# Inverse square roots of an attention kernel's norms: one GpSimd power in place of VectorE's Newton rounds

## What is computed

```python
def rmsnorm(x, g, eps=EPS):                      # cross-attention, D = 128
    var = jnp.mean(jnp.square(x), axis=-1, keepdims=True)
    return x * jax.lax.rsqrt(var + eps) * g
q = rmsnorm((hidden @ Wq).reshape(B, Sq, 16, 128), gq)
k = rmsnorm((context @ Wk).reshape(B, 257, 16, 128), gk)
...
def rms_norm(x):                                 # self-attention, 16 numbers a head
    return x * jax.lax.rsqrt(jnp.mean(x * x, axis=-1, keepdims=True) + RMS_EPS)
q, k = (rms_norm(q), rms_norm(k))                # 16 + 4 heads = 20 norms a row
```

## Time and profile before

| | before |
|---|---|
| median of 3 runs | 1631.33 us |
| profiled execution, its own time | 1639.87 us |
| its span | 1638.0 us |
| PE busy | 1413.0 us, 86% |
| DVE busy | 1067.2 us, 65% |
| ACT busy | 866.7 us, 53% |
| POOL busy | 543.6 us, 33% |
| mean granted TensorE clock | 0.928 |

### The profile page before, as it was taken

The page is one execution under the profiler, slowest core; times in us unless marked ns, Lnnn a source line. Parts: engine busy times, 40 slices in busy tenths (PEclk is TensorE's granted clock), DMA queues, the critical chain, the costliest instruction groups (busy, mean ns, idle before and its releaser), DMA issues.

```text
span 1638.0 us, 32905 instructions
## 1 busy us (share of the span) xinstructions
PE 1413.0 (86%) x9178; PEld 988.4 (60%) x9178; DVE 1067.2 (65%) x3905; ACT 866.7 (53%) x3432; POOL 543.6 (33%) x1338
## 2 busy tenths in 40 slices
PE   5859989999999998989989999999998989955872
PEld 2635757575756666565757575756666665735661
DVE  7737677776768586767777676768586767733112
ACT  4455556556665556565555566665656565521110
POOL 2243343334242425243343334242425243310003
PEclk9989899999999999999898999999999989876896
DMA  9000000000000001010000000000001000100534
GB/s 368 4 24 8 22 20 20 13 26 14 23 17 14 26 10 30 7 30 9 20 20 20 13 24 17 23 17 23 16 10 29 9 28 6 58 6 9 170 125 131
DMA packets 41214, 59.83 MB, mean 37 GB/s; under 512 B 5094, under 2 KB 35953, under 8 KB 40096
## 3 DMA queue, kind: packets, MB, share of 16 engines
q1 hardware_dynamic: 36880, 50.73, 9.8%
q0 software_dynamic: 2064, 6.14, 1.1%
q10 hardware_dynamic: 2176, 2.10, 0.4%
HBM read 48.62 MB, written 10.49 MB: 36 GB/s over the span
## 4 chain that ended last, share of the span: by engine, by line
PE 46%; issue 26%; POOL 12%; ACT 7%; DVE 4%; DMA 3%; POOLq 1%; SPq 0%; DVEq 0%; ACTq 0%
PE AB L587 21%; PE Eb L587 9%; PE Db L587 5%; PE C L704 3%; PE C L587 3%; ACT px L1003 2%; POOL prob L1140 2%; DMA ctxn<-expert_rows 2%; PE AB L783 2%; POOL c_lo L1105 2%; PE C L720 2%; ACT AB L924 2%; POOL pjunk L1099 1%; POOL rstd L1116 1%; POOL rkx L1131 1%
## 5 line engine op out<-in xcount | busy, mean ns | idle before, releaser
L924 ACT ACTIVATE AB<-AB 128x128 f32<-128x128 f32 (+1 forms) x1160 | 303.0, 261 | 203.4 <-PE AB L587 198.6
L1099 POOL TENSOR_TENSOR pjunk<-pjunk 128x1 f32<-128x1 f32 x288 | 57.3, 199 | 653.8 <-DVE sinv L1443 383.6
L1281 DVE BATCH_NORM_STATS2 kst<-AB 128x6 f32<-128x256 f32 x512 | 181.9, 417 | 83.3 <-PE AB L587 49.4
L924 ACT ACTIVATION_READ_ACCUMULATOR AB<-AB 128x1 f32 (+1 forms) x1160 | 215.8, 186 | 0.0
L587 PE MATMUL AB<-wk_hi,c_hi 128*128 128x512 f16 x512 | 203.7, 398 | 11.2 <-DVE wvo_lo L1354 2.9
L587 PE MATMUL AB<-wk_lo,c_hi 128*128 128x512 f16 x512 | 201.9, 394 | 0.0
L587 PE MATMUL AB<-wk_hi,c_lo 128*128 128x512 f16 x512 | 201.0, 393 | 0.0
L993 ACT ACTIVATE prob<-prob,nbias,rq 128x257 f32<-128x257 f32 x256 | 150.7, 591 | 39.8 <-DVE nbias L1438 39.4
L587 PE MATMUL AB<-ctxT,qpT 128*128 128x257 f32 x512 | 140.7, 422 | 0.6 <-DVE kst L1281 0.6
L1140 POOL TENSOR_SCALAR prob<-prob,sinv 128x257 f32<-128x257 f32 x256 | 125.0, 488 | 20.1
L1116 POOL TENSOR_TENSOR rstd<-var,minus_half 128x1 f32<-128x1 f32 x64 | 35.5, 555 | 266.6 <-DVE var L1266 232.1
(11 more groups left out here) (253 smaller groups left out, 3278.0 us busy)
## 6 DMA issues: line engine op xcount, KB each, us to landing
ctxT<-in_ctxT SPq DMA_DIRECT2D x64, 128.5 KB, 2.1
ctxn<-in_ctxn SPq DMA_DIRECT2D x64, 128.0 KB, 2.1
wq_hi<-in_w SPq DMA_DIRECT2D x4, 768.0 KB, 5.2
wq_lo<-in_w SPq DMA_DIRECT2D x4, 768.0 KB, 6.5
expert_rows<-base POOLq DMA_DIRECT2D x1, 2048.0 KB, 15.8
xin<-in_x SPq DMA_DIRECT2D x16, 128.0 KB, 2.2
prob<-in_wqT SPq DMA_DIRECT2D x1, 2048.0 KB, 19.7
xres<-in_x SPq DMA_DIRECT2D x16, 128.0 KB, 2.0
```

The lines of the kernel that those rows point to most:

```text
L924: ins = nc.scalar.activation(k, k, ACT.Square, accum_out=sums[0:m, h:h + 1])
L1099: own.mark(pool.tensor_tensor(pjunk[:, 0:1], pjunk[:, 1:2], pjunk[:, 1:2], ALU.mult))
L1281: ins = V.bn_stats(stats[:, 0, 2 * half + n], AB[0:m, 2 + half, 2 * D * n:2 * D * (n + 1)])
```

## The change

`newton` and its scratch tiles go. DVE still makes mean square plus epsilon, now into tiles of their own (`nk`, `nq`, `nqk`), and signals `norm_ready`. POOL takes it to the power -0.5 in one `tensor_tensor` against a tile filled with -0.5, in four new steps: `p0` and `p1` (128 x 64 each), `pq` (128 x 16) and `pk` (128 x 20); in the first period also one of 64 x 16 in `rkl`. DVE's `RQ` is cut in two: what follows the inverse root (the 16 copies) is the new step `rq`, which waits for `pq` and stands behind `f` (in the first period behind `tw`). `qkv` is cut in the same way; `qr` follows it at once and waits for `pk`.

```diff
 ORDER = {
-    "DVE": """K0 X K1 K2 dp3 XL K3 KN0 do3 Q RQ f K4 K5 qkv K6 s0 sc K7 i0 s1 KN1 pt dp0 i1 pv s2 pr ln2 dp1 lg i2
+    "DVE": """K0 X K1 K2 dp3 XL K3 KN0 do3 Q RQ f rq K4 K5 qkv qr K6 s0 sc K7 i0 s1 KN1 pt dp0 i1 pv s2 pr ln2 dp1 lg i2
               do0 up pos do1 s3 dn dp2 i3 do2""".split(),
-    "POOL": """h0 h1 n3 h2 X cl r0 ln1 c1 c0 r1 c2 h3 n0 r2 n1 y c3 ln2 r3 n2 scat""".split(),
+    "POOL": """h0 h1 n3 h2 X cl p0 r0 pq ln1 c1 c0 r1 c2 h3 pk n0 p1 r2 n1 y c3 ln2 r3 n2 scat""".split(),
 START_ORDER = {
-    "DVE": """low wk KL KNL K0 K1 X K2 XL wql K3 gg KN0 Q W0l wt0 W1l K4 RQ wt1 M01 wt K5 M23 tw s0 s1 i0 K6 dp0
+    "DVE": """low wk KL KNL K0 K1 X K2 XL wql K3 gg KN0 Q W0l wt0 W1l K4 RQ wt1 M01 wt K5 M23 tw rq s0 s1 i0 K6 dp0
-    "POOL": """hl h1 h3 h2 h0 rkl X r0 pz r1 cl c0 n0 c1 n1 r2 c2 r3 n2 c3""".split(),
+    "POOL": """hl h1 h3 h2 h0 rkl X p0 r0 pz pq r1 cl c0 n0 c1 n1 p1 r2 c2 r3 n2 c3""".split(),
...
+            def inverse(p, name, out, src):
+                pool.wait_ge(norm_ready.sem, norm_ready.at(p, name))
+                m, n = src.shape
+                ins = pool.tensor_tensor(out, src, minus_half[0:m, 0:n], ALU.pow)
+                if name in ("RQ", "qkv"):
+                    ins.then_inc(inv_ready.sem, 1)
+                else:
+                    own.mark(ins)
...
-                step(V.tensor_scalar(na[0:m, 0:n], src, 1.0 / (D * WK_SCALE ** 2), X_EPS, ALU.mult, ALU.add))
-                newton(n, out, m).then_inc(rk_ready.sem, 1)
+                V.tensor_scalar(out, src, 1.0 / (D * WK_SCALE ** 2), X_EPS, ALU.mult, ALU.add).then_inc(norm_ready.sem, 1)
...
-                step(newton(H, rqt[:]))
+            def step_rq(p):
+                dve.wait_ge(inv_ready.sem, inv_ready.at(p, "pq"))
                 for b in range(NB):
                     for m in range(4):
...
-                step(newton(NQK, qki[:]))
+            def step_qr(p):
+                dve.wait_ge(inv_ready.sem, inv_ready.at(p, "pk"))
                 step(V.tensor_tensor(qki[:, 0:AH], qki[:, 0:AH], again[:], ALU.mult))
```

More of the change, by code:

```diff
@@ L57 @@
 N_CONST = sum(CONSTS.values())
-DVE_STEPS = dict(pro=80, full=89, last=38, expert=0)
-POOL_STEPS = dict(pro=37, full=40, last=5, expert=0)
+DVE_STEPS = dict(pro=35, full=43, last=26, expert=0)
+POOL_STEPS = dict(pro=40, full=42, last=5, expert=0)
 class Period:
@@ L147 @@
 LATE = {"n3", "ph3", "tl3", "oh3", "pt3", "o3", "dp3", "do3", "f", "ln1", "xt1", "qkv", "qk", "sc", "pt", "pv", "y", "yt", "pr",
-        "ln2", "xt2", "lg", "up", "pos", "dn", "scat"}
+        "ln2", "xt2", "lg", "up", "pos", "dn", "scat", "qr", "pk"}
 ORDER = {
@@ L218, in build @@
         ones = sb("ones", [P, P])
-        minus_half = sb("minus_half", [P, 1])
+        minus_half = sb("minus_half", [P, NB * H])
         wq_hi = sb("wq_hi", [P, KC, INNER], F16)
@@ L328, in build @@
         na = sb("na", [P, NB * H])
-        nb_ = sb("nb_", [P, NB * H])
-        nc_ = sb("nc_", [P, NB * H])
+        nk = sb("nk", [P, 2, NB * H])
+        nq = sb("nq", [P, H])
+        nqk = sb("nqk", [P, AH + AKV])
         tscale = sb("tscale", [P, 10], BF16)
@@ L380, in build @@
                              full=entries("POOL", FULL, "h"))
-        rk_ready = Events(sem("rk_ready"), pro=steps_among("DVE", PRO, ["KNL", "KN0", "KN1"]),
-                          full=steps_among("DVE", FULL, ["KN0", "KN1"]))
+        norm_ready = Events(sem("norm_ready"), pro=steps_among("DVE", PRO, ["KNL", "KN0", "KN1", "RQ"]),
+                            full=steps_among("DVE", FULL, ["KN0", "KN1", "RQ", "qkv"]), last=["qkv"])
+        inv_ready = Events(sem("inv_ready"), pro=["pq"], full=steps_among("POOL", FULL, ["pq", "pk"]), last=["pk"])
         rq_ready = Events(sem("rq_ready"), **fills)
@@ L1115, in rsqrt @@
                 pool.wait_ge(var_ready.sem, var_ready.at(p, name))
-                pool.tensor_tensor(rstd[:, n:n + 1], var[:, n:n + 1], minus_half[:], ALU.pow)\
+                pool.tensor_tensor(rstd[:, n:n + 1], var[:, n:n + 1], minus_half[:, 0:1], ALU.pow)\
                     .then_inc(rstd_ready.sem, 1)
+            def inverse(p, name, out, src):
[6 more added lines that the diff above has]
+                    own.mark(ins)
             def spread(p, b):
-                pool.wait_ge(rk_ready.sem, rk_ready.at(p, "KN0" if b < 2 else "KN1"))
                 if p.kind == "pro":
@@ L1200, in step_rkl @@
             def step_rkl(p):
-                pool.wait_ge(rk_ready.sem, rk_ready.at(p, "KNL"))
+                inverse(p, "KNL", rkl[:], nk[0:BATCH, 1, 0:H])
+                own.settle()
                 pool.tensor_copy(rkx[0:BATCH, 0, 0].rearrange("p (h q) -> p h q", q=SQ),
@@ L1206, in _ @@
                      "ln2": lambda p: rsqrt(p, "ln2", 3), "pz": step_pz, "scat": scatter,
-                     "hl": step_hl, "rkl": step_rkl, "cl": split_last}
+                     "hl": step_hl, "rkl": step_rkl,
+                     "p0": lambda p: inverse(p, "KN0", all_of(rk[:, 0:NB]), nk[:, 0]),
+                     "p1": lambda p: inverse(p, "KN1", all_of(rk[:, NB:2 * NB]), nk[:, 1]),
+                     "pq": lambda p: inverse(p, "RQ", rqt[:], nq[:]), "pk": lambda p: inverse(p, "qkv", qki[:], nqk[:]), "cl": split_last}
             for b in range(NB):
@@ L1244, in gate @@
                 own.mark(V.memset(junk[:], 0.0))
[L1246 to L1258, removed]
             def layer_norm(p, name, n, x, out, free=None):
@@ L1305, in step_KN @@
                 n = NB * H
-                key_norms(p, P, n, kst[:, NB * part:NB * (part + 1)], kn2[:, n * part:n * (part + 1)], all_of(rk[:, NB * part:NB * (part + 1)]),
-                          f"KN{part}")
+                key_norms(p, P, n, kst[:, NB * part:NB * (part + 1)], kn2[:, n * part:n * (part + 1)], nk[:, part], f"KN{part}")
             def step_X(p):
@@ L1323, in step_RQ @@
                 sums_from_stats(P, qst[:], 1, qn2[:])
-                step(V.tensor_scalar(na[:, 0:H], qn2[:], 1.0 / (D * WQ_SCALE ** 2), X_EPS, ALU.mult, ALU.add))
-                step(newton(H, rqt[:]))
+                V.tensor_scalar(nq[:], qn2[:], 1.0 / (D * WQ_SCALE ** 2), X_EPS, ALU.mult, ALU.add).then_inc(norm_ready.sem, 1)
+            def step_rq(p):
+                dve.wait_ge(inv_ready.sem, inv_ready.at(p, "pq"))
                 for b in range(NB):
@@ L1471, in step_qkv @@
                 step(V.tensor_reduce(qkn[:], qk2[:].rearrange("p (h n) -> p h n", n=AD), AX.X, ALU.add))
-                step(V.tensor_scalar(na[:, 0:NQK], qkn[:], 1.0 / AD, A_EPS, ALU.mult, ALU.add))
-                step(newton(NQK, qki[:]))
+                V.tensor_scalar(nqk[:], qkn[:], 1.0 / AD, A_EPS, ALU.mult, ALU.add).then_inc(norm_ready.sem, 1)
+            def step_qr(p):
+                dve.wait_ge(inv_ready.sem, inv_ready.at(p, "pk"))
                 step(V.tensor_tensor(qki[:, 0:AH], qki[:, 0:AH], again[:], ALU.mult))
@@ L1595, in step_dn @@
                 V.tensor_tensor(base[:], x2[:], Eb[:, 0:DIM], ALU.add).then_inc(drained["E"].sem, 1)
-            steps = dict(X=step_X, XL=step_XL, Q=lambda p: key_stats(p, "Q", P, qst), RQ=step_RQ,
+            steps = dict(X=step_X, XL=step_XL, Q=lambda p: key_stats(p, "Q", P, qst), RQ=step_RQ, rq=step_rq, qr=step_qr,
                          wql=step_wql, W0l=lambda p: step_Wl(p, 0), W1l=lambda p: step_Wl(p, 1), f=step_f, qkv=step_qkv, sc=step_sc, pv=step_pv,
@@ L1602, in _ @@
                          low=step_low, wk=step_wk, wt0=step_wt0, wt1=step_wt1, wt=step_wt2, gg=step_gg, tw=step_tw, KL=lambda p: key_stats(p, "KL", BATCH, kst_last),
-                         KNL=lambda p: key_norms(p, BATCH, H, kst_last, knl[:], rkl[:], "KNL"),
+                         KNL=lambda p: key_norms(p, BATCH, H, kst_last, knl[:], nk[0:BATCH, 1, 0:H], "KNL"),
                          M01=lambda p: wvo_low(p, 0), M23=lambda p: wvo_low(p, 1))
```

## The result

| | before | after |
|---|---|---|
| median | 1630.26 us (4 runs) | 1890.37 us (4 runs, 1885.96 to 1893.25) |
| ratio after / before | | 1.155, 95% interval 1.150 to 1.161 |
| span of the profiled execution | 1638.0 us | 1888.3 us |
| PE busy | 1413.0 us | 1477.1 us |
| PE idle (span less busy) | 225.0 us | 411.2 us |

The account below looks back on a forecast made before the run. TensorE's ordered work was taken to set the end. Fifteen periods at 1.48 us later, less 1.1 us once, gave +21: 1661 us against the profiled execution, 1652 us as a median; range 1608 to 1760 us.

Parts of the forecast that it names:

- the powers: GpSimd's inverse roots: 0.03 us a column, so 2.4 us for 64 columns, between bounds of 0.69 and 23.0 us.
- forecast A: Copies held up 4 to 6 us, powers cheap: `qkv` 1.48 us later a period, 1637 to 1670 us; chance 0.38.
- rival C: Wide powers dear, so GpSimd late for `ln1` and `rk2`: 1751 us, up to about 2230 us; chance 0.24.
- the prediction's last sentence: A TensorE clock that changes with the moved waits would disturb the sum either way; no size given.
- The free allowance of 4.9 us: Key-norm powers on GpSimd: up to 4.9 us for 64 columns, the choice of length costs nothing.
- do3 and f: `do3` runs as soon as ScalarE is done, so TensorE starts `f` 0.85 us earlier a period.
- f to xt1: VectorE's `f` no longer queues behind copies, so the 0.88 us wait at `xt1` goes; lead so far 1.73 us.
- The copies: The 16 copies, now before `K4`'s sums, stretch beside GpSimd's run from 2.8 to 5.0 us and delay `qkv`.
- The rule of the Trainium skill: GpSimd and some VectorE instructions share SBUF ports, one fully blocking the other; taken strictly, some 36 us over before.
- `p0` makes RQ's sums wait: VectorE's query-norm sums, with two SBUF inputs, wait beside the key power `p0`, hidden under TensorE's `f`.
- qkv: Small-head norms: 2.35 us of Newton become 1.1 us of power plus 0.12 hand-over; 1.1 us gained once, last period.
- What would show it: Signs against: copies in 2.8 us, or a 128 x 64 power over 5 us with TensorE waiting at `xt1` and `rk2`.

Follow-up runs that it names:

- e1: The changed kernel with each wide power replaced by a subtraction of the same tiles, inverse root left out: 1626.9 us, 0.998 of before.
- e6: The kernel before with only `do3` moved ahead of a Newton block of the key norms on VectorE: 1624.5 us, 0.996 of before.
- e12: e10 plus one unread 128 x 64 GpSimd power each full period, ahead of the context-column split that TensorE needs: 1731.5 us, 1.062 of before.
- e10: The kernel before, Newton kept, with `do3` earlier and the 16 copies on ScalarE: 1577.4 us, 0.964 of before.
- e3: The changed kernel with only the key norms by power; query and small-head norms by Newton, copies as before: 1762.9 us, 1.082 of before.
- e8: The changed kernel, all powers kept, with the 16 copies moved behind `K5` on VectorE: 1872.1 us, 1.151 of before.
- e4: e1 (subtraction for each power) with the 16 copies moved behind `K5` on VectorE: 1575.1 us, 0.965 of before.
- e5: The kernel before, Newton kept, with `do3` earlier and the 16 copies behind `K5` on VectorE: 1626.0 us, 0.997 of before.
- e7: e5 with the query norms by one 128 x 16 GpSimd power instead of Newton: 1613.6 us, 0.991 of before.
- e13: e12 with the unread power one step later, behind the context-column split: 1581.3 us, 0.971 of before.

## Why the prediction was wrong, by its own steps

- **The step that failed: the powers, "I take 0.03 us a column".** Measured 0.16. I read the excess of the 128 x 1 power over a product, 0.356 us, as mostly a latency paid once; the line through four widths gives 0.16 us of it again for every column. The bounds, 0.69 and 23.0 us for 64 columns, held (10.56); the value stood near the lower one because a product's slope was near, and a product says nothing of a power's. It moves the sum by the 13.3 us a period of the next point, where forecast A had 1.48. The error was to choose among ends 33 times apart by a row of another operation, and to cut the range at 1760 us although rival C reached 2230.
- **Rival C's arithmetic holds with the measured length.** `xn1` is done at 755.53 + 10.56 + 1.4 + 2.9 + 0.56 + 0.6 = 771.5, the copies at 776.5, `qkv` starts at 778.5, 7.6 us late; `r2` at 707.27 + 10.55 + 1.4 = 719.2, 5.7 us late. 15 x 13.3 = 199 us of idle time; measured 186.2. By places it is less exact. In the first half PE waits 2.28 + 2.94 + 2.68 us, less the 1.73 us that went, so 6.2 us net for 7.6; in the second half it waits 6.1 to 6.8 us for 5.7. The two differences partly cancel, which is luck. PE's wait at `rk0` is in no list of the prediction. What the sum had no term for is the clock, 64.1 us more of busy PE; the prediction's last sentence names it as something that could disturb the sum.
- **The free allowance of 4.9 us**, which is the room of `p1`, stood in the text and fits: `p1` passes it by 5.7 us and PE waits 6.1 to 6.8 us. No run here tried a key power near it.
- **do3 and f: right, f to xt1: right but for the powers.** In e1 neither wait is left in the stretch of the earlier trace rows; in the changed kernel the one at `f` is gone and the one at `xt1` is 2.7 us, by `p0` and `pq` ahead of `ln1`. By e6 both moves are needed: `do3` early alone takes away 0.85 us at `f` and adds 1.5 us at `xt1`.
- **The copies: right.** Forecast 5.0 us, measured 5.22, and PE then waits inside `K5` for K4's sums. Forecast A by itself is e1: idle time as summed, +18.2 for +21, but the clock gives back 17.0. So A's own conditions give "no change" and not 1652 us: that part of the forecast would have missed too.
- **The rule of the Trainium skill, SBUF — State Buffer, section "SBUF: two separate sides"**: the product of 1.00 us beside a `c_lo` of 0.67 us agrees with it, and the copies nearly do (16 of them in 5.22 us beside fourteen short instructions, where one each would take 6.0). A power of 10.56 us with 128 x 320 two-input products of 0.48 us beside it does not. The measurement decides: VectorE is not held out for the whole of a power. The prediction's remark that `p0` makes RQ's sums wait is wrong with it: they take their usual 0.17 us beside `p0` (878.04 above).
- **qkv: wrong in sign.** Forecast 1.1 + 0.12 us; DVE waits 3.67 us for `pk`, longer than the 2.35 us that Newton took. In the last period, the one place where this counted, PE waits 8.3 us for the heads, where it was to fall from 7.0 by 1.1; with a subtraction (e1) it waits 5.0.
- **What would show it** named the rows that appeared: a 128 x 64 power over 5 us, and PE waiting on POOL at `rk2`.

## What to carry to other kernels

An operation seen at one width in a trace has no known price at another: before an engine takes over eleven cheap instructions in one, measure that one at the width it will have, or keep the whole bound in the range. A long instruction on an idle engine costs what is queued behind it: 10.6 us were free behind the last needed step and cost 154 us in all one step earlier. Look first at short helper work that stands ahead of a critical step; moving 16 small copies into gaps of a third engine, together with `do3` (0.4% by itself), gained 3.6% with no arithmetic changed.

## What was not expected of the hardware

- A GpSimd power of 64 columns takes 10.56 us, 33 times a subtraction of the same size (0.315 us), and its cost does not depend on whether 64 or 128 partitions take part (2947 and 2905 ns for 16 columns).
- The price of an idle PE can be more than the idle time, and it is not in proportion to it. e12 has 95.6 us more idle time than e10 and 63.3 us more busy time for the same matmuls; the clock goes from 0.954 to 0.903. After against before: 186.2 and 64.1. But e3 against before: 108.0 us more idle time and only 8.7 more busy time. In the other direction, e10 against before has 24.8 us less idle time and 37.5 us less busy time. Which of PE's short waits decide the clock is open; it was not tried.
- The 32 x 4 copies take 161 ns each in the kernel before and 169 in e8, 312 beside GpSimd's run of short instructions (e1), 204 to 222 behind `K5` in e4, e5 and e7, and 206 on ScalarE.
- VectorE runs two-input products at their usual 0.48 us beside a GpSimd power that reads SBUF, and at 1.00 us beside a GpSimd product of 0.67 us. Only the first 0.2 us or so of a power may hold it up (e13, 0.65 us).
